# A two-layer graph network on one core: late sums cut to ten positions, the first block mixed behind the fifth sum, a loop count loaded ahead

## What is computed

```python
h = jnp.maximum(_layernorm(x, axis=-1), 0.0)
x1 = h[src].reshape(-1, 16, 32)            # 16 segments of 32
x2 = edge_attr_512.reshape(-1, 16, 32)
i1, i2, i3 = path_indices[:, 0], path_indices[:, 1], path_indices[:, 2]    # 64 paths
contrib = path_coeffs[None, :, None] * x1[:, i1, :] * x2[:, i2, :]
edge_out = zeros.at[:, i3, :].add(contrib)
x = x + zeros.at[dst].add(edge_out.reshape(-1, 512))
```

## Time and profile before

| | us |
|---|---|
| median of three runs | 1072.91 |
| lowest, highest | 1070.64, 1081.23 |
| the profiled execution | 1072.47 |
| its span, first to last instruction | 1070.8 |
| VectorE busy | 897.5 |
| TensorE busy (matmuls) | 829.7 |
| GpSimd busy | 492.3 |
| ScalarE busy | 444.3 |
| mean granted TensorE clock | 0.878 |

### The profile page before, as it was taken

How to read it: one execution, slowest core, us unless ns; L and a number is a source line. 1 busy time by engine, 2 the same in 40 slices (tenths; PEclk the granted TensorE clock), 3 DMA queues, 4 the chain that set the end, 5 groups by cost and what they waited for, 6 DMA issues and landing times.

```text
span 1070.8 us, 22798 instructions
## 1 busy us (share of the span) xinstructions
PE 829.7 (77%) x5046; PEld 394.0 (37%) x5053; DVE 897.5 (84%) x2196; ACT 444.3 (41%) x1685; POOL 492.3 (46%) x572
## 2 busy tenths in 40 slices
PE   1688887996167787868788987878797787887878
PEld 0343443442022443524243443424344243443426
DVE  4677668843069999999999999899998999999894
ACT  3888887432401523425161432416133261522423
POOL 4211220443634546566454657546564564646400
PEclk9999999998578898898889888888987889888788
DMA  9000000043555656687665657666565775767610
GB/s 166 1 0 0 0 0 2 15 192 124 165 229 204 229 177 238 233 284 249 240 239 187 235 195 275 255 219 245 188 233 195 254 256 182 247 188 241 225 21 10
DMA packets 59517, 183.03 MB, mean 171 GB/s; under 512 B 20116, under 2 KB 20244, under 8 KB 54972
## 3 DMA queue, kind: packets, MB, share of 16 engines
q0 software_dynamic: 27616, 87.97, 26.1%
q1 hardware_dynamic: 22568, 88.88, 22.3%
q10 hardware_dynamic: 9268, 5.55, 1.9%
HBM read 173.71 MB, written 8.66 MB: 170 GB/s over the span
## 4 chain that ended last, share of the span: by engine, by line
PE 26%; DVEq 21%; DVE 20%; issue 17%; ACT 6%; POOL 4%; DMA 2%; ACTq 1%; SPq 1%; another core or an unknown queue 1%; POOLq 0%
DVE q_mem L858 16%; PE psum L1226 15%; DVEq L850 10%; DVEq L853 5%; PE psum L1211 4%; DVEq L858 4%; PE psum L1129 3%; ACT S L1059 3%; PE psum L1140 2%; DVE x_mem L748 2%; ACT hot_mem L1046 2%; DMA x_mem<-in_L_gnn_W 1%; PE psum L1126 1%; POOL x_mem L622 1%; POOL spare L515 1%
## 5 line engine op out<-in xcount | busy, mean ns | idle before, releaser
L858 DVE TENSOR_TENSOR q_mem<-x_mem 128x448 f32 (+2 forms) x1392 | 725.6, 598 | 68.3 <-DMA x_mem<-h_rows,src_now 31.6
L1226 PE MATMUL psum<-q_mem,hot_mem 128*32 128x512 f32 x2584 | 424.4, 714 | 136.6 <-DVE q_mem L858 79.4
L622 POOL DMA_INDIRECT x_mem<-h_rows,src_now x323 | 390.8, 1210 | 174.3 <-issue 94.5
L1059 ACT ACTIVATE S<-psum,coef 128x32 f32<-128x32 f32 (+1 forms) x800 | 147.5, 335 | 301.4 <-issue 133.6
L1226 PEld LDWEIGHTS psum<-q_mem,hot_mem 128*32 128x32 f32 x2584 | 107.5, 126 | 414.5 <-issue 294.1
L1211 PEld LDWEIGHTS psum<-S,place 128*128 128x128 f32 x1600 | 187.8, 194 | 45.9 <-issue 45.7
L1211 PE MATMUL psum<-S,place 128*128 128x32 f32 x1600 | 195.2, 278 | 11.8 <-issue 11.5
L748 DVE TENSOR_SCALAR x_mem<-x_mem,spare 128x320 bf16<-128x320 f16 x323 | 77.8, 299 | 42.0 <-issue 42.0
L1071 ACT ACTIVATE acc<-psum 128x512 f32<-128x512 f32 x12 | 7.2, 597 | 201.4 <-PE psum L1211 201.4
L1140 PE MATMUL psum<-x_mem,hot_mem 128*128 128x320 bf16 x323 | 67.2, 321 | 28.8 <-DVE x_mem L748 20.3
L953 ACT ACTIVATE hot_mem<-x_mem,spare 128x128 bf16<-128x128 f16 x240 | 74.9, 388 | 20.5 <-PE psum L1140 20.0
(11 more groups left out here) (187 smaller groups left out, 437.8 us busy)
## 6 DMA issues: line engine op xcount, KB each, us to landing
x_mem<-in_edge_attr SPq DMA_DIRECT2D x60, 768.0 KB
x_mem<-in_edge_attr SPq DMA_DIRECT2D x35, 1024.0 KB
x_mem<-h_rows,src_now POOLq DMA_INDIRECT x323
out<-acc POOLq DMA_DIRECT2D x12, 256.0 KB, 4.3
x_mem<-in_x SPq DMA_DIRECT2D x1, 2304.0 KB
out<-x_mem ACTq DMA_DIRECT2D x9, 256.0 KB
h_rows<-x_mem ACTq DMA_DIRECT2D x9, 256.0 KB, 2.0
x_mem<-in_L_gnn_W SPq DMA_DIRECT2D x1, 1024.0 KB, 13.9
```

The source lines that it names most:

```text
L622: pool.indirect_dma_start(x1[:, j * TB + t, :], None, h2_dram[:, :], bass.IndirectOffsetOnAxis(ap=now, axis=0)).then_inc(landed, 16)
L858: return nc.vector.tensor_tensor(q[s % 2][:, 0:tiles, p % PG:p % PG + 1, :], x1_segs[:, first:first + tiles, ds(a, 1), :], x2_segs[:, firs ...
L1059: last = nc.scalar.activation(S[:, p * U:(p + 1) * U], sums, ACT.Copy, scale=coef[:, p:p + 1])
L1226: last = nc.tensor.matmul(ps[s % G][side * M:(side + 1) * M, :], hot[:, j * TB + k, :], q[s % 2][:, k, :, :].rearrange("p n u -> p (n u)") ...
```

## The change

It has three parts. TensorE's sum of the last block covers ten positions (`EDGE`, 320 columns); the other six stand in a matmul group of their own behind a branch that is taken when `kept_n` is over 58. Block 0 is mixed behind slot 4, the fifth sum, and not behind slot 5, in all items. And VectorE loads the next item's loop count behind the products of slot 4 and no longer between two items.

```diff
+    EDGE = 10
-    MIX_AT, MIX_LAST = {1: [G - 1], 0: [G - 2], G + 1: [0], 2 * G - 1: [1]}, {1: [G - 1], 0: [G - 2], G + 1: [0], G + 2: [1]}
+    MIX_AT, MIX_LAST = {1: [G - 1], 0: [G - 2], G: [0], 2 * G - 1: [1]}, {1: [G - 1], 0: [G - 2], G: [0], G + 2: [1]}
...
-            def product_turn(again, turn):
+            def product_turn(again, turn, next_item):
...
                     for g in range(G):
                         product_slot(turn, j * G + g, g, j * TB, n)
+                        if j and g == 0:
+                            many_next = item_turn_count(next_item)
+                return many_next
...
+            def item_turn_count(item):
+                return dve.value_load(meta[0:1, TURNS + item:TURNS + item + 1], min_val=1, max_val=WINDOWS * PLACES)
...
+            kept_n = pe.value_load(n_kept, min_val=SURE, max_val=NP)
...
-                for t in range(max(b - a for a, b in cut)):
-                    for side, (a, b) in enumerate(cut):
-                        if t < b - a:
-                            k = at[side] + t
-                            last = nc.tensor.matmul(ps[s % G][side * M:(side + 1) * M, :], hot[:, j * TB + k, :],
-                                                    q[s % 2][:, k, :, :].rearrange("p n u -> p (n u)"),
-                                                    start=(j == 0 and t == 0), stop=(j == 1 and t == b - a - 1))
-                last.then_inc(summed, 1)
+
+                def add(first, end):
+                    for t in range(max(b - a for a, b in cut)):
+                        for side, (a, b) in enumerate(cut):
+                            if t < b - a:
+                                k = at[side] + t
+                                last = nc.tensor.matmul(ps[s % G][side * M:(side + 1) * M, first * U:end * U], hot[:, j * TB + k, :],
+                                                        q[s % 2][:, k, first:end, :].rearrange("p n u -> p (n u)"),
+                                                        start=(j == 0 and t == 0), stop=(j == 1 and t == b - a - 1))
+                    return last
+
+                if s % G < G - 1:
+                    add(0, PG).then_inc(summed, 1)
+                else:
+                    with pe.If(kept_n > NP - PG + EDGE):
+                        add(EDGE, PG)
+                    add(0, EDGE).then_inc(summed, 1)
```

More of the change, by code:

```diff
@@ L895, in product_last @@
                         product_slot(turn, j * G + g, g, j * TB, n)
-            for item in range(ITEMS - 1):
-                product_turns(dve, item, turn_count, product_turn)
-            product_turns(dve, ITEMS - 1, turn_count, product_last)
+            def item_turn_count(item):
+                return dve.value_load(meta[0:1, TURNS + item:TURNS + item + 1], min_val=1, max_val=WINDOWS * PLACES)
+            many = item_turn_count(0)
+            for item in range(ITEMS):
+                with dve.Fori(0, many) as again:
+                    turn = dve.snap(turn_count, min_val=0, max_val=ITEMS * WINDOWS * PLACES - 1)
+                    if item < ITEMS - 1:
+                        many_next = product_turn(again, turn, item + 1)
+                    else:
+                        product_last(again, turn)
+                    dve.reg_add(turn_count, turn_count, 1)
+                many = many_next
             total = dve.snap(**all_placed(turn_count))
```

## The result

The changed kernel takes 1138.09 us in the median of four runs (1131.01 to 1141.56); the kernel before took 1071.85 beside it. The ratio is 1.0589, with a 95% interval of 1.0511 to 1.0668: slower, by more than forecast. The profiled execution took 1131.01 us, the lowest of the four; its span is 1129.3 us, 58.5 more than before. The medians are 66.2 us apart, so some 8 us of the loss lie in executions that no trace shows.

The account below looks back on a forecast made before the run. VectorE's products were taken to bound the kernel. From 1072.5 us, new waits +44.4, old turn-start waits -11, waits before the second half +6, tail -1 and shrinking holes -2 gave +36.4, 1109 us; range 1090 to 1124.

Parts of the forecast that it names:

- slot 7: VectorE's products of the last block in a turn's second half (slots count from 0): new wait, 3.7 us a turn.
- Slot 0's wait: VectorE at each turn's first block, waiting for TensorE's seventh sum: the old 0.92 us wait goes.
- the restart of VectorE: From the end of TensorE's sixth sum to VectorE's first product of the last block: 0.65 us.
- 5.2, exactly what leads to 0.50: TensorE's sixth sum, behind 3.0 us idle and 4 us narrow work: starts at the slow clock, takes 5.2 us.
- The turn starts: VectorE ahead of each turn's first block: eleven old waits gone, 1.0 us each, -11 us in all.
- Slots 4 and 5: VectorE at the second half's first two blocks: a wait before the first, 0.5 us on average, +6 us in all.
- The tail: Last item's end: its last sum has fewer columns ahead of two mixes, -1 us.
- slots 1 to 3: VectorE at the first half's later blocks: larger holes in a few turns shrink, -2 us.
- A: Rival: TensorE's clock stays fast through block 0's mix and the sixth sum; 1072 us, chance 0.06.
- B: Rival: chain from fifth sum to last block's products fits VectorE's two slots, no new wait; 1060 us, chance 0.05.
- C: Rival: the narrower late sums pay in full on VectorE, 30 us less, 1042 us; chance 0.01.
- D: Rival: the late-sum branch is taken after all, doubling a late sum's matmuls; 1110 us, chance 0.01.

Follow-up runs that it names:

- mix_only: Kernel before with one edit, block 0 mixed behind the fifth sum of a turn: 1129.46 us, ratio 1.0797.
- late_sums_only: Kernel before with only the narrower late sums and their branch: 1046.97 us beside 1046.24, ratio 1.0006.
- filled_wide: Changed kernel with whole-array filler matmuls, five behind the fifth sum and three within the mix of block 0: 1100.09 us, ratio 1.0493.
- base_again: Kernel before, unchanged, traced on a chip of the experiments: one execution of 1050.75 us.
- mix_skip: Changed kernel without the 32 narrow matmuls of block 0's mix, wait for the save and zeroing kept: 1067.1 us beside 1059.66, ratio 1.0056.
- split_no_load: Kernel before with narrower late sums and branch, block 0 mixed in halves behind the sixth and seventh sums, two fillers in the first: ratio 0.9964.
- split: Changed kernel with block 0 mixed in halves behind the sixth and seventh sums, two fillers in the first: ratio 1.0008.

## Why the prediction was right in its mechanism and wrong in its size

**What held.** The place and the cause: slot 7 waits for sum 5, which stands behind the save and the mix (mix_only 1.0797, late_sums_only 1.0006). The late sums take 2.35 us fast, as worked out, and without the move they pay nothing. The branch isn't taken. Slot 0's wait is gone: 0.06 to 0.09 us in most turns against 0.92. Slot 4 has the new wait of 0.5 to 0.7 us in nine turns. The turn period is 67.2 us, (1041.82 - 369.73)/10 from the starts of slot 0, where 64.9 was forecast.

**What failed** is the size of three terms of the chain: the mix, sum 5 and the restart of VectorE. The means over the 12 turns of the changed kernel's trace, beside the terms of the prediction:

| | predicted, us | measured, us |
|---|---|---|
| sum 4 | 5.5 | 5.4 |
| save of block 0 | 3.0 | 3.2 |
| zeroing and mix 0 | 5.5 | 6.4 |
| sum 5 | 5.2 | 5.9 |
| from its end to VectorE's first product | 0.65 | 1.1 |
| sum | 19.9 | 22.0 |
| two slots of VectorE | 16.1 | 16.1 |
| wait ahead of slot 7 | 3.7 | 5.85 |

I took the mix as half slow and sum 5 as long as sum 6 was before, 5.3 us, which has one slow stretch at its start. But sum 6 came directly behind a mix that had run fast. Sum 5 now comes behind a wait and a mix that has already run slow for over 4 us, and the clock stays at 0.50 over nearly all of it: in the stretches from 618.6 to 628.6 it doesn't rise. Sum 5 takes 6.5 us there and 6.3 to 6.5 in eight of the twelve turns. In the eighth and the tenth turn the mix was slow from end to end, 7.0 us behind a sum 4 of 6.0, and the wait was 8.1 and 7.9 us. My step "5.2, exactly what leads to 0.50" had the cause and stopped at one stretch. The restart has nothing to do with the clock, since it is 1.0 us in the fast turns of filled_wide too. I had read its 0.65 us at slot 0, which has no branches ahead of its first product. In the kernel before, slot 7's branches ran from 602.69 on, before the last products of slot 6 had started, and now they wait for the sum as well. With 70.2 us of these waits in place of 44.4 the term is short by 26, 5 of them by the restart.

The other terms, on the spans (1070.8 and 1129.3 us, 58.5 apart). The turn starts gave back 8.7 us, not 11. Slots 4 and 5 cost 2.6, not 6, since the kernel before had 3.5 us of waiting there already. The tail costs 6.4 more where I had 1 less: I took sum 7's columns off and did not ask what clock the two mixes behind it would get; they took 13.87 us at mostly 1.2 GHz. And slots 1 to 3 waited 12.0 us less, where I had 2: their holes are gone. That is luck, and without it I would have been 10 us further off. base_again, where the kernel before has no such holes, shows that they are no property of the kernel alone. They made it slower on the first chip, which is part of why the loss is 5.9% there and 7.4% on the other. Together, 69.7 ahead of slot 7 (it had 0.4 before) - 8.7 + 2.6 + 6.4 - 12.0 is 58.0 of the 58.5.

The bounds, 1090 to 1124 us, were too narrow for the same reason. I had 6.5 us as the largest wait of a turn, and 4.7 as the largest mean; single turns have 8.1, since three terms are slow at once. They were treated as if they varied apart, but it is one clock, and mix and sum 5 lie in the same slow stretch.

**The rivals.** A, the clock staying fast, is what filled_wide makes true by force in 7 of 12 turns; the changed kernel never has it. I had cited for it the Trainium skill, "TensorE: Matmul & The Clock Gate", section "What's actually happening", by which the gate follows how busy TensorE has been. The engine's busy row doesn't tell that much here: in 618.6 to 621.8 TensorE is busy all of the time with 32-column matmuls and stays at 0.50, while the same mix with wide matmuls in and ahead of it runs at 1.00 in 7 of 12 turns. B, that the chain fits, is nearly reached only without the mix (mix_skip). C is out by late_sums_only. D, the branch taken after all, is out too: TensorE has the same 5046 matmuls as before.

**The load.** I priced it at 0 to 0.5 us and took 0. It seems to be worth 0.65 us a turn in the changed kernel, and only there: mix_only has 0.72 ahead of most slots 0, the changed kernel 0.06. The two differ in the late sums as well, so this is argued and not shown. In the trace of the kernel before, VectorE's queue loads the count at 608.17, when two products of slot 7 have yet to start, and the load hides in that lead. split_no_load, which has no wait ahead of slot 7, has the load in its old place and none ahead of ten of its eleven slots 0. Behind a wait ahead of slot 7 the lead is gone, and the load shows. Alone the load ahead made the kernel 0.9% slower, which no row of before foretold.

## What to carry to other kernels

When a step is moved ahead on an engine that works in order, add up the whole chain from its new place to the next work that someone waits for, with the producer's time in it (here a save of 2.97 us) and not the step's own time alone, and hold it against the time that the waiting engine has. Where the clock of an engine depends on what it did before, its terms don't vary apart: take all of them slow together for the bound, and ask of each slow stretch how many of the next terms lie in it. And read the restart of a waiting engine at the place where it will wait, with what its queue has to do there. A gain that is taken out of one wait often shows in the next one (split), so a variant that does its work in the trace still has to be timed.

## What the hardware showed that was not expected

With 32-column matmuls TensorE stayed at 1.2 GHz although it was busy without a gap (618.6 to 621.8: 3.20 of 3.20 us at 0.50), and the 512-column sum behind them took up to 6.5 us and not 3.6. Behind a wait of 3.1 us and no mix it took up to 6.6. With wide fillers, three in a mix of 3.8 us and five ahead of it, mix and sum ran at 2.4 GHz in 7 of 12 turns. One wide filler with a short bf16 one cost 2.9%. Behind a wait VectorE's first product came 1.0 us after the sum where five branches stood ahead of it in the queue, and 0.5 where none did. A register load of 0.5 us on VectorE, moved to where little waited for it (0.2 us in three turns), changed the time by 0.9%. And in the kernel before, holes of 2.3 to 2.5 us were there in one trace and in none of another chip's.
